# Attention output in transposed form: values stationary in four column groups, probabilities normalised before they stream

## The chip, the cores and the metric

The kernel runs on one core of one Trainium2 chip. Its time is the device time in microseconds; before, the median of three runs is 1509.24 us (1506.75 to 1510.07). Engines: PE (TensorE), DVE (VectorE), ACT (ScalarE), POOL (GpSimd), and SP, whose queue issues the large DMAs.

## What is computed

64 graphs of 128 nodes with 384 features, and one weighted 128x128 adjacency matrix each. Layer 0 is an attention with 12 heads of 32 channels, layer 1 is a graph network of two inner layers. Cut to what matters:

```
h = maximum(layernorm(x), 0)
q, k = h @ Wq.T, h @ Wk.T ;  v = h @ Wv.T + bv          # 12 heads of 32
s = q k^T * 384**-0.5 + 2 * adj
s = where(any(s != 0 in the row), s, -inf)
p = nan_to_num(softmax(s))
x = x + (p v) @ Wo.T + bo
h = maximum(layernorm(x), 0)
for l in 0, 1:
    u = h W_l h^T / sqrt(384), one matrix left of the diagonal's side, another on the other side
    delta = exp(u) * adj
    ctx = (delta / (sum(delta) + 1e-10)) @ (h @ W_lin.T + b_lin)
    h = relu(layer_norm(ctx))
x = x + h
```

## The kernel before, in words

Two graphs (j = 0, 1) form a group of 256 tokens; 32 groups follow each other. Every matrix product of full size is made from two parts: an operand is held as a high part and a low remainder, and three products (high-high, high-low, low-high) are summed in PSUM. So each PSUM result is read twice, by ACT, which writes the high part (L483), and by DVE, which subtracts it and writes the low part (L585).

The steps of one group, by name: T1a, T1b transpose the normed input; QK0 to QK2 give queries and keys, V0, V1 the values; S{j}{a} are scores, four row groups a of 32 rows each, three heads in each; x{j}{a} are the exponentials of S{j}{a} on ACT (L507), 3 of 128x128 each; ph{j}{b} and pl{j}{b} split half b of the probabilities into two float16 parts (L515, L697); pth, ptl are DMA transposes of these parts on SP's queue; PV{j} multiplies them with the values (L415); OT{j} transposes the result (L422); WO{j} is the output projection. Then ln2, T2a, T2b, and for each inner layer l: N{l}0 to N{l}2 (six 256-column products in three steps), HL{l}{j}, U{l} (the scores), the chain U{l}.m, .w, .e, .d, .dh, .dl that makes delta and its two parts on DVE and ACT, C{l}{j} (the product with delta, which needs delta's low part), gst and gag (statistics), z, and HTa, HTb (transposes to the next inner layer).

The order on each engine is written by hand in the table ORDER: a row (step, ahead) says for which group a step is done while group g is at hand. Each engine works through its list strictly in that order, for g = 0 to 31. So attention of group g+1 runs beside the graph network of groups g and g-1. PSUM has eight banks, and BANK says which steps share one, in turn; a PE step waits until the step before it in its bank is drained.

Before, the exponentials stay unnormalised. PV{j} has the turned probabilities as its stationary operand (128x128) and streams 33 columns for each head: 32 values and a column of ones, whose result is the row's sum. DVE then takes the reciprocal of 12 sums (PV.r, PV.n) and scales (PV.o, L689), into o_sb, with nodes in the partitions; OT turns it. `prob`, the float32 buffer of the exponentials, exists once and serves j = 0 and j = 1 in turn.

Of the kernel before, what the change touches and what calls it, by code (L numbers as in the profile page):

```python
# [61 lines left out]
def w_lin(l):  # L62
# [9 lines left out]
    0: ["N12", "S00", "HL00", "QK2"],  # L72
    1: ["HL11", "C11", "T1a", "U0", "V1"],
    2: ["WO1", "T2a", "S10", "QK0", "WO0"],
    3: ["N10", "S03", "S12", "QK1", "HTa"],
    4: ["HL10", "S02", "S11", "PV0", "PV1", "HTb"],
    5: ["N11", "S01", "N02", "HL01", "OT0", "OT1"],
    6: ["T2b", "AT", "C10", "N00", "T1b", "C00"],
    7: ["U1", "N01", "S13", "C01", "V0"],
# [791 lines left out]
```

## Time and profile before

| | us |
|---|---|
| median of 3 runs | 1509.24 |
| the profiled execution, own time | 1507.34 |
| its span, first to last instruction | 1505.4 |
| PE busy | 1432.3 |
| DVE busy | 1243.8 |
| ACT busy | 903.5 |
| POOL busy | 508.9 |

Busy times are the union of an engine's instructions. The timelines used below merge instructions that follow each other: the first number is the start, the second the length. Instructions of one engine overlap a little at their ends, so what a step costs its engine is the distance from its start to the next start, where no idle time is noted in brackets.

### The profile page before, as it was taken

The page shows a single profiled execution, that of the slowest core. Times are in us where ns is not written, and L with a number is a line of the kernel's source. Part 1 is how long each engine was busy: PE and PEld are TensorE (multiplying, and loading weights), DVE is VectorE, ACT ScalarE, POOL GpSimd, SP SyncE. Part 2 cuts the span into 40 slices and gives each one's busy share as a digit, 9 for nine tenths or more (in the row PEclk, how much of TensorE's full clock was granted, in tenths as well). Part 3 has the DMA queues.
Part 4 walks back from the last instruction along what each step waited for, and adds up shares of the span by engine and source line. Part 5 has one row for each costly group of instructions (what it writes and reads, how often), then busy time and mean ns, then how long its engine had stood idle before and what let it go on. Part 6 is the DMA issues. An engine that isn't in the chain of part 4 may idle for free.

```text
span 1505.4 us, 40241 instructions
## 1 busy us (share of the span) xinstructions
PE 1432.3 (95%) x14464; PEld 1396.4 (93%) x14464; DVE 1243.8 (83%) x4619; ACT 903.5 (60%) x2027; POOL 508.9 (34%) x921
## 2 busy tenths in 40 slices
PE   3699999999999999999999999999999999999874
PEld 3599999999999999999999999999999999999874
DVE  5578988888888888888888888888888888888853
ACT  4566665656666556666565666656666665566531
POOL 4113333233334233343323333333333342333321
PEclk8799999999999999999999999999999999999996
DMA  6232322223221223232222333222223222232200
GB/s 216 54 57 58 68 42 62 48 64 68 57 62 43 55 60 64 58 67 50 55 50 61 68 57 68 41 57 53 64 68 57 56 49 57 58 64 57 54 12 11
DMA packets 235683, 89.39 MB, mean 59 GB/s; under 512 B 206784, under 2 KB 235200, under 8 KB 235488
## 3 DMA queue, kind: packets, MB, share of 16 engines
q1 hardware_dynamic: 234912, 85.63, 26.9%
q8 instruction: 119, 1.95, 0.5%
q0 software_dynamic: 576, 1.18, 0.3%
q14 instruction: 76, 0.62, 0.2%
HBM read 23.86 MB, written 12.58 MB: 24 GB/s over the span
## 4 chain that ended last, share of the span: by engine, by line
PE 92%; DVE 2%; DMA 2%; ACT 1%; issue 1%; POOL 1%; SPq 0%; DVEq 0%; POOLq 0%; ACTq 0%
PE bank L342 79%; PE bank L348 4%; PE bank L415 4%; PE bank L403 3%; PE bank L422 1%; DMA x_sb<-x 1%; DMA pT<-prob_parts 1%; PE bank L434 0%; ACT prob L507 0%; SPq L323 0%; DVE weights L570 0%; ACT xn L490 0%; DVE stats_ln L598 0%; ACT prob_parts L515 0%; ACT work L556 0%
## 5 line engine op out<-in xcount | busy, mean ns | idle before, releaser
L342 PE MATMUL bank<-h,weights 128*128 128x256 f32 x3456 | 425.1, 280 | 3.0 <-DVE h L750 3.0
L342 PEld LDWEIGHTS bank<-h,weights 128*128 128x128 f32 x3456 | 411.9, 190 | 3.8 <-issue 3.7
L507 ACT ACTIVATE prob<-prob,rmin 128x128 f32<-128x128 f32 x768 | 244.2, 393 | 3.4 <-DVE rmin L665 3.4
L342 PE MATMUL bank<-weights,h 128*128 128x384 f32 x1152 | 227.5, 342 | 0.0
L342 PE MATMUL bank<-hA,weights 128*128 128x256 f32 x1728 | 219.2, 283 | 1.4 <-DVE hA L585 1.4
L342 PEld LDWEIGHTS bank<-hA,weights 128*128 128x128 f32 x1728 | 212.1, 190 | 1.7 <-DVE hA L585 1.7
L342 PEld LDWEIGHTS bank<-weights,h 128*128 128x128 f32 x1152 | 194.3, 188 | 6.3
L483 ACT ACTIVATE n<-bank 128x512 fp32r<-128x512 f32 x192 | 113.7, 592 | 141.7 <-PE bank L342 141.0
L800 POOL TENSOR_SCALAR less_mean_gnn<-mv_gnn 128x2 f32<-128x2 f32 x64 | 32.9, 513 | 429.9 <-DVE mv_gnn L590 429.9
L665 DVE CUSTOM_DVE_ANT_0 prob<-bank,adj_sb 128x128 f32<-128x128 f32 x768 | 171.0, 286 | 0.2 <-issue 0.2
L585 DVE TENSOR_TENSOR n<-bank,n 128x512 fp32r<-128x512 f32 x192 | 128.9, 684 | 33.8 <-ACT n L483 28.9
L342 PE MATMUL bank<-n,h 128*128 128x256 f32 x1152 | 153.1, 287 | 0.3 <-DVE n L585 0.3
L342 PEld LDWEIGHTS bank<-n,h 128*128 128x128 f32 x1152 | 142.0, 191 | 1.0 <-issue 1.0
L787 POOL TENSOR_SCALAR less_mean_ln<-mv_ln 128x2 f32<-128x2 f32 x64 | 20.7, 324 | 358.0 <-DVE mv_ln L590 358.0
L697 DVE TENSOR_TENSOR prob_parts<-prob,prob_parts 128x768 f16<-128x768 f32 x128 | 118.2, 943 | 5.7 <-ACT prob_parts L515 5.6
L342 PE MATMUL bank<-weights,oT 128*128 128x384 f32 x576 | 115.8, 346 | 0.3 <-DVE oT L585 0.3
L342 PE MATMUL bank<-weights,hA 128*128 128x384 f32 x576 | 115.8, 345 | 0.0
L515 ACT ACTIVATE prob_parts<-prob 128x768 f16<-128x768 f32 x128 | 108.0, 844 | 3.1
L820 POOL TENSOR_TENSOR x_sb<-x_sb,bo_all 128x384 f32<-128x384 f32 x64 | 69.5, 1087 | 115.1 <-ACT xn L490 109.8
L342 PEld LDWEIGHTS bank<-weights,oT 128*128 128x128 f32 x576 | 101.2, 190 | 0.5 <-issue 0.5
L585 DVE TENSOR_TENSOR hl<-bank,hl 128x384 fp32r<-128x384 f32 x128 | 70.6, 552 | 34.2 <-ACT hl L483 34.2
L342 PEld LDWEIGHTS bank<-weights,hA 128*128 128x128 f32 x576 | 97.4, 188 | 0.0
(101 smaller groups left out, 2453.8 us busy)
## 6 DMA issues: line engine op xcount, KB each, us to landing
x_sb<-x SPq DMA_DIRECT2D x32, 384.0 KB, 3.2
out<-x SPq DMA_DIRECT2D x32, 384.0 KB, 2.7
adj_sb<-adj SPq DMA_DIRECT2D x32, 128.0 KB, 2.1
pT<-prob_parts SPq DMA_TRANSPOSE x256, 2.8
x<-w SPq DMA_DIRECT2D x3, 576.0 KB, 4.8
pT<-w SPq DMA_DIRECT2D x3, 576.0 KB, 6.6
prob<-w SPq DMA_DIRECT2D x2, 576.0 KB, 7.3
prob_parts<-w SPq DMA_DIRECT2D x2, 576.0 KB, 6.0
```

The costliest lines, as they stand in the source:

```text
L342: mm = pe.matmul(out, lhsT, rhs, start=(n == 0), stop=(n == len(pairs) - 1))
L348: mm = pe.transpose(bank(job)[:, n * T + j * P:n * T + (j + 1) * P], src[:, j, c * P:(c + 1) * P], ident[:, :])
L403: mm = pe.matmul(bank(f"S{j}{a}")[:, c * P:(c + 1) * P], qk[rs, g % 2, u, c, js], qk[rs, g % 2, v, C + c, js], start=(n == 0), stop=(n == ...
L415: mm = pe.matmul(bank(step)[:, h * DA:(h + 1) * DA], pT[:, a, h % HC * C + h // HC, :], v2[:, b, j, h, :], start=(h == 0 and n == 0), stop ...
L483: act.activation(out, src, ACT.Copy).then_inc(s_hi, 1)
L507: e = act.activation(prob[:, a * C + h // HC, :], prob[:, a * C + h // HC, :], ACT.Exp, bias=rmin[:, j, h:h + 1], scale=-1.0)
L515: act.activation(pp[:, HI, hs, :], prob[:, hs, :], ACT.Copy).then_inc(s_part[HI][b], 1)
L585: dve.tensor_tensor(out, src, hi_part if hi_part.dtype == F16 else hi_part.bitcast(F32), ALU.subtract).then_inc(free(job), 1)
L665: r = dve.tensor_tensor_reduce(prob[:, a * C + c, :], bank(step)[:, c * P:(c + 1) * P], adj_sb[:, p, j, :], -2.0, 3.0e38, ALU.add, ALU.min ...
L697: dve.tensor_tensor(pp[:, LO, hs, :], prob[:, hs, :], pp[:, HI, hs, :], ALU.subtract).then_inc(s_part[LO][b], 1)
L800: pool.tensor_scalar(less_mean["gnn"][:, :], mv["gnn"][:, :, 0], -1.0, None, ALU.mult)
L820: pool.tensor_tensor(x_sb[:, p, j, :], x_sb[:, p, j, :], bo_all[:, :], ALU.add).then_inc(s_xbo[j], 1)
```

## The change

PV{j} is turned round. The values of a head (128x32) become the stationary operand, written to 32 of the 128 PSUM partitions, so that the four heads a of one c occupy four column groups; the turned probabilities stream, 128 columns. The result has channels in the partitions, which is the form that OT made, so OT{j} is left out; ACT and DVE split the PV result straight into oT. As the sum of a row can't be applied to this form afterwards, the probabilities are scaled before: each exponential also writes its sum (accum_out), DVE's new step nr{j}{b} takes the reciprocals of six sums, and ph{j}{b} first scales six 128x128 tiles on ACT, waits for them, and then writes the high part. The scale carries a factor -128, which the weight Wo takes back. The column of ones goes. The tables BANK and ORDER are new throughout.

```diff
@@ BANK, ORDER, SPLIT_AFTER: new tables; one line of the SP list
-        ("ld_x", 2), ("ld_adj", 2), ("pth01", 1), ("pth00", 1), ("ptl00", 1), ("ptl01", 1), ("pth10", 1), ("ptl10", 1),
+        ("ld_x", 2), ("ld_adj", 2), ("pth01", 1), ("ptl01", 1), ("pth00", 1), ("ptl00", 1), ("pth10", 1), ("ptl10", 1),
...
@@ PE
-                    for h in range(NH):
-                        for n, (a, b) in enumerate(PARTS):
-                            mm = pe.matmul(bank(step)[:, h * DA:(h + 1) * DA], pT[:, a, h % HC * C + h // HC, :], v2[:, b, j, h, :],
-                                           start=(h == 0 and n == 0), stop=(n == 2), skip_group_check=True)
-                    mm.then_inc(full(step), 1)
-                elif step[:2] == "OT":
-                    j = int(step[2])
-                    wait_drained(pe, f"PV{j}", g)
+
                     for c in range(C):
-                        mm = pe.transpose(bank(step)[:, c * P:(c + 1) * P], o_sb[:, j, c * P:(c + 1) * P], ident[:, :])
+                        for n, (u, w) in enumerate(PARTS):
+                            for a in range(HC):
+                                mm = pe.matmul(bank(step)[a * D:(a + 1) * D, c * P:(c + 1) * P], v2[:, w, j, c * HC + a, :], pT[:, u, a * C + c, :],
+                                               start=(n == 0), stop=(n == len(PARTS) - 1))
                     mm.then_inc(full(step), 1)
...
@@ ACT
-                        e = act.activation(prob[:, a * C + h // HC, :], prob[:, a * C + h // HC, :], ACT.Exp, bias=rmin[:, j, h:h + 1], scale=-1.0)
+                        e = act.activation(prob[:, a * C + h // HC, :], prob[:, a * C + h // HC, :], ACT.Exp, bias=rmin[:, j, a * C + h // HC:a * C + h // HC + 1], scale=-1.0,
+                                           accum_out=exp_sum[:, j, a * C + h // HC:a * C + h // HC + 1])
                     e.then_inc(s_exp[j][a], 1)
                 elif step[:2] == "ph":
                     j, b = int(step[2]), int(step[3])
                     hs = slice(2 * b * C, 2 * (b + 1) * C)
-                    for a in (2 * b, 2 * b + 1):
-                        act.wait_ge(s_exp[j][a], g + 1)
+                    act.wait_ge(s_nrm[j][b], g + 1)
+                    for i in range(2 * b * C, 2 * (b + 1) * C):
+                        e = act.activation(prob[:, i, :], prob[:, i, :], ACT.Copy, scale=rinv[:, j, i:i + 1])
+                    e.then_inc(s_scaled[j][b], 1)
                     ge(act, s_turned[HI][b], 16 * (G * g + j))
+                    act.wait_ge(s_scaled[j][b], g + 1)
                     act.activation(pp[:, HI, hs, :], prob[:, hs, :], ACT.Copy).then_inc(s_part[HI][b], 1)
...
@@ DVE
-                elif step[:2] == "PV":
...
+                elif step[:2] == "nr":
+
+                    j, b = int(step[2]), int(step[3])
+                    hs = slice(2 * b * C, 2 * (b + 1) * C)
+                    dve.wait_ge(s_row0[j], g + 1)
+                    for a in (2 * b, 2 * b + 1):
+                        dve.wait_ge(s_exp[j][a], g + 1)
+                    dve.scalar_tensor_tensor(out=row0[:, j, hs], in0=exp_sum[:, j, hs], scalar=float(P), in1=row0[:, j, hs],
+                                             op0=ALU.is_equal, op1=ALU.mult)
+                    dve.reciprocal(rinv[:, j, hs], exp_sum[:, j, hs]).then_inc(s_recip[j][b], 1)
+                    dve.wait_ge(s_recip[j][b], g + 1)
+                    dve.scalar_tensor_tensor(out=rinv[:, j, hs], in0=row0[:, j, hs], scalar=-P_SCALE, in1=rinv[:, j, hs],
+                                             op0=ALU.add, op1=ALU.mult).then_inc(s_nrm[j][b], 1)
```

What the new order does at two places. First PE, from U0 to HTb. Before, U0 is the block into bank1 from n2, then come PV0, QK0, QK1, and the two C blocks (hl, dT):

```order
L342 MATMUL bank1<-n2,h0 128x256 x18
L415 MATMUL bank4<-v2,pT 128x33 x36
L342 MATMUL bank2<-hA,weights 128x256 x18
L342 MATMUL bank3<-hA,weights 128x256 x18
L342 MATMUL bank6<-hl,dT 128x386 x3
L342 MATMUL bank7<-hl,dT 128x386 x3
L342 MATMUL bank0<-hA,weights 128x256 x18
L422 MATMUL bank5<-ident,o_sb 128x128 x3
```

After, PE from U0 (bank6 from n2), QK0, PV0, C01, C00, QK2, QK1, V0, WO0, PV1:

```order
L346 MATMUL bank6<-n2,h0 128x256 x18
L346 MATMUL bank2<-hA,weights 128x256 x18
L421 MATMUL bank4<-pT,v2 32x128 x36
L346 MATMUL bank1<-hl,dT 128x386 x3
L346 MATMUL bank7<-hl,dT 128x386 x3
L346 MATMUL bank6<-hA,weights 128x256 x18
L346 MATMUL bank1<-hA,weights 128x256 x18
L346 MATMUL bank5<-weights,hA 128x384 x9
L346 MATMUL bank3<-weights,oT 128x384 x9
L421 MATMUL bank1<-pT,v2 32x128 x36
```

Between U0 and the C blocks there is one QK block now where there were two; the OT transposes are gone.

The second place is ACT, the steps of graph j = 1. Before, from x{1}{.} to the splits of the QK blocks, the exponentials stand in threes between other steps:

```order
L507 ACTIVATE prob<-prob,rmin 128x128 x3
L483 ACTIVATE hl<-bank5 128x384
L483 ACTIVATE hA<-bank6 128x256
L507 ACTIVATE prob<-prob,rmin 128x128 x3
L515 ACTIVATE prob_parts<-prob 128x768
L507 ACTIVATE prob<-prob,rmin 128x128 x3
L540 ACTIVATE work<-work 128x256
L507 ACTIVATE prob<-prob,rmin 128x128 x3
L515 ACTIVATE prob_parts<-prob 128x768
```

After, on ACT, from x12 to ph11; L515 are now the scale copies and L519 the high parts:

```order
L507 ACTIVATE prob,exp_sum<-prob,rmin 128x128 x3
L483 ACTIVATE hA<-bank2 128x256
L483 ACTIVATE hl<-bank1 128x384
L554 ACTIVATE c_sb<-c_sb,shift_gnn,scale_gnn 128x384 x2
L483 ACTIVATE hA<-bank5 128x512
L507 ACTIVATE prob,exp_sum<-prob,rmin 128x128 x9
L483 ACTIVATE hl<-bank3 128x384
L545 ACTIVATE work<-work 128x256
L515 ACTIVATE prob<-prob,rinv 128x128 x6
L519 ACTIVATE prob_parts<-prob 128x768
L515 ACTIVATE prob<-prob,rinv 128x128 x6
L519 ACTIVATE prob_parts<-prob 128x768
```

Both ph steps have moved behind the last exponential, since their scales need the sums, and each has six scale copies ahead of it. On DVE, the order from U0 on is now U0.m, r01, U0.w, nr10, nr11, HL01, U0.d, U0.dh, U0.dl; before, it had no step there that needs an exponential other than pl10.

On DVE before, the steps after U1 are U1.m, U1.w, S01, U1.d, U1.dh, HL11, U1.dl, S03, S02, S00. After, they are U1.m, U1.w, S02, T2b, U1.d, S01, U1.dh, S03, U1.dl, HL11, S00, r00, nr01, N01, C11, nr00, C10, gst11, gst10, pl01, gag1, S12, S13, pl00, N02, N00, S11, S10, T1b, T1a, HL00. ACT's list beside it, after T2b and xn1_1: U1.e, x02, HL11, AT, x01, x03, N01, x00, ph01, ph00, N02, N00, x12, T1b, HL00, z1_0, z1_1, T1a, x11, x10, x13, HL01, U0.e, ph10, ph11.

## Rows read from the trace of the kernel before

**Rows 1.** The page: busy time by engine, and the chain by engine.

```profile
PE 1432.3 (95%) x14464; PEld 1396.4 (93%) x14464; DVE 1243.8 (83%) x4619; ACT 903.5 (60%) x2027; POOL 508.9 (34%) x921
...
PE 92%; DVE 2%; DMA 2%; ACT 1%; issue 1%; POOL 1%; SPq 0%; DVEq 0%; POOLq 0%; ACTq 0%
```

**Rows 2.** Windows view: 20 groups; clock, DMA share and GB/s come last.

```profile
300.00:1185.60 885.60, 884.50 (x9040) 865.15 (x9039) 765.73 (x2881) 555.39 (x1260) 313.51 (x560) 1.00 0.28 58
```

**Rows 3.** Timeline of PE: start us, us, engine, line, operation, count.

```profile
709.14 1.07 PE L415 MATMUL bank<-v,pT 128*128 128x33 f16 x36
710.06 4.49 PE L342 MATMUL bank<-hA,weights 128*128 128x256 f32 x36
...
717.57 0.49 PE L422 MATMUL bank<-ident,o_sb 128*128 128x128 f32 x3
717.82 1.82 PE L342 MATMUL bank<-weights,hA 128*128 128x384 f32 x9
...
736.79 0.68 PE L403 MATMUL bank<-qk 32*128 32x128 f16 x36
737.40 1.83 PE L342 MATMUL bank<-weights,h 128*128 128x384 f32 x9
...
753.39 1.06 PE L415 MATMUL bank<-v,pT 128*128 128x33 f16 x36
```

**Rows 4.** Timeline of ACT, the stretch with AT, x, splits, z1, ph.

```profile
740.26 0.38 ACT L530 ACTIVATE adjT<-bank 128x256 f32<-128x256 f32 x1
740.53 2.74 ACT L507 ACTIVATE prob<-prob,rmin 128x128 f32<-128x128 f32 x9
743.16 0.58 ACT L483 ACTIVATE n<-bank 128x512 fp32r<-128x512 f32 x1
743.64 0.84 ACT L515 ACTIVATE prob_parts<-prob 128x768 f16<-128x768 f32 x1
...
749.68 1.31 ACT L549 ACTIVATE c_sb<-c_sb,shift_gnn,scale_gnn 128x384 f32<-128x384 f32 x2 [1.84 <-POOL shift_gnn L809]
750.89 0.47 ACT L483 ACTIVATE hl<-bank 128x384 fp32r<-128x384 f32 x1
751.27 0.98 ACT L507 ACTIVATE prob<-prob,rmin 128x128 f32<-128x128 f32 x3
...
752.52 0.37 ACT L483 ACTIVATE hA<-bank 128x256 fp32r<-128x256 f32 x1
```

**Rows 5.** Timeline of DVE: PV1.r and PV1.n; U1.m to U1.dl; HL01.

```profile
720.66 0.17 DVE L680 SCALAR_TENSOR_TENSOR row<-bank,row 128x12 f32<-128x12 f32 x1 [0.90 <-PE bank L415]
...
721.01 0.17 DVE L685 SCALAR_TENSOR_TENSOR rinv<-row,rinv 128x12 f32<-128x12 f32 x1
...
737.00 0.69 DVE L724 TENSOR_TENSOR work<-bank,mask 128x512 f32<-128x512 f32 x1 [0.43 <-PE bank L342]
737.72 0.43 DVE L727 TENSOR_TENSOR work<-work 128x256 f32<-128x256 f32 x1
738.07 0.28 DVE L665 CUSTOM_DVE_ANT_0 prob<-bank,adj_sb 128x128 f32<-128x128 f32 x1
...
738.71 0.42 DVE L730 TENSOR_TENSOR work<-work,adjT 128x256 f32<-128x256 f32 x1
739.16 0.29 DVE L733 CAST dT<-work 128x256 fp32r<-128x256 f32 x1
...
740.28 0.41 DVE L736 TENSOR_TENSOR dT<-work,dT 128x256 fp32r<-128x256 f32 x1
...
752.17 0.55 DVE L585 TENSOR_TENSOR hl<-bank,hl 128x384 fp32r<-128x384 f32 x1
```

**Rows 6.** Groups by line and shape: busy us, mean ns.

```profile
L515 ACT ACTIVATE prob_parts<-prob 128x768 f16<-128x768 f32 x128 | 108.0, 844 | 3.1
...
L665 DVE DVE_READ_ACCUMULATOR2_ANT rmin<- 128x1 f32 x768 | 63.9, 83 | 0.0
...
L502 ACT ACTIVATE v<-v_sum 128x384 f16<-128x384 f32 x64 | 33.7, 527 | 30.9 <-DVE v_sum L654 30.9
```

More of the change, by code:

```diff
@@ L51 @@
 WQ, WK, WV, WO = range(4)
+P_SCALE = 128.0
+W_SCALE = {WQ: Q_SCALE, WK: K_SCALE, WO: -1 / P_SCALE}
 def w_left(l):
@@ L71 @@
 BANK = {
[L72 to L79, printed above, removed]
+    0: ["S03", "S11"],
+    1: ["WO1", "U1", "C10", "HL00", "C01", "QK1", "PV1"],
+    2: ["S01", "T1b", "QK0"],
+    3: ["N11", "T2a", "HL11", "C11", "S13", "HL01", "WO0"],
+    4: ["S02", "N02", "PV0", "HTb"],
+    5: ["N10", "N12", "T2b", "N01", "S12", "T1a", "V0", "HTa"],
+    6: ["HL10", "S00", "N00", "U0", "QK2"],
+    7: ["AT", "S10", "C00", "V1"],
 }
@@ L83 @@
     "SP": [
[1 row of a table removed]
[1 row of a table added]
         ("pth11", 1), ("ptl11", 1), ("out", -1)],
     "PE": [
[5 rows of a table removed]
-    "ACT": [
[5 rows of a table removed]
[5 rows of a table added]
+    "ACT": [
[5 rows of a table added]
         ("HTa", 0)],
     "DVE": [
[9 rows of a table removed]
[9 rows of a table added]
     "POOL": [
-        ("ln2", 0), ("ln1", 2), ("xbo0", 2), ("ml", 0), ("xbo1", 2), ("gn1", -1), ("mu", 0), ("za0", -1), ("za1", -1),
-        ("zb0", -1), ("zb1", -1), ("gn0", 0)],
+        ("ln2", 0), ("ln1", 2), ("xbo0", 2), ("mu", 0), ("ml", 0), ("xbo1", 2), ("gn1", -1), ("za0", -1), ("za1", -1),
+        ("zb1", -1), ("zb0", -1), ("gn0", 0)],
 }
 SPLIT_JOBS = (["T1a", "T1b", "QK0", "QK1", "QK2",
-              "OT0", "OT1", "T2a", "T2b"] + [f"N{l}{k}" for l in range(L) for k in range(3)] +
+              "PV0", "PV1", "T2a", "T2b"] + [f"N{l}{k}" for l in range(L) for k in range(3)] +
               [f"HL{l}{j}" for l in range(L) for j in range(G)])
@@ L168, in build @@
         v_sum = sb("v_sum", [P, G, H])
-        v2 = sb("v2", [P, 2, G, NH, DA], F16)
+        v2 = sb("v2", [P, 2, G, NH, D], F16)
         prob = sb("prob", [P, NH, P])
@@ L177, in build @@
         row0 = sb("row0", [P, G, NH])
+        exp_sum = sb("exp_sum", [P, G, NH])
         rinv = sb("rinv", [P, G, NH])
@@ L223, in build @@
         s_row0 = [sem(f"row0_{j}") for j in range(G)]
-        s_recip = [sem(f"sum_inverse{j}") for j in range(G)]
-        s_rinv = [sem(f"negated_inverse{j}") for j in range(G)]
+        s_recip = [[sem(f"sum_inverse{j}{b}") for b in range(2)] for j in range(G)]
+        s_nrm = [[sem(f"prob_scale{j}{b}") for b in range(2)] for j in range(G)]
+        s_scaled = [[sem(f"prob_scaled{j}{b}") for b in range(2)] for j in range(G)]
         s_mask = [sem("mask_left"), sem("mask_right")]
@@ L245, in build @@
         SPLIT_AFTER = {
-            "ACT": {"": (0,), "xn1_1": (1,), "T1b": (2, 3), "QK1": (4, 5), "QK0": (6,), "QK2": (7,), "V0": (8,), "V1": (9,)},
-            "DVE": {"ln1_ag": (0,), "T1b": (1, 2), "QK1": (3, 4), "QK0": (5,), "QK2": (6, 7), "V0": (8,), "V1": (9,)}}
+            "ACT": {"": (0,), "xn1_1": (1,), "T1a": (2, 3), "QK0": (4, 5), "QK2": (6,), "QK1": (7,), "V0": (8,), "V1": (9,)},
+            "DVE": {"ln1_ag": (0,), "T1a": (1, 2), "QK0": (3, 4), "QK2": (5,), "QK1": (6, 7), "V1": (8,), "V0": (9,)}}
         def staged(m):
@@ L412, in run @@
                             pe.wait_ge(s_turned[part][b], 16 * (G * g + j + 1))
[L413 to L420 removed]
                     for c in range(C):
[L422 removed]
+                        for n, (u, w) in enumerate(PARTS):
+                            for a in range(HC):
+                                mm = pe.matmul(bank(step)[a * D:(a + 1) * D, c * P:(c + 1) * P], v2[:, w, j, c * HC + a, :], pT[:, u, a * C + c, :],
+                                               start=(n == 0), stop=(n == len(PARTS) - 1))
                     mm.then_inc(full(step), 1)
                 elif step[:2] == "WO":
[L425 removed]
+                    wait_drained(pe, f"PV{step[2]}", g)
                     rows(step, g, WO, oT, 0)
@@ L475, in split_weights @@
                     wait_load(act, m)
-                    act.activation(W[:, m, HI, :, :], staged(m), ACT.Copy, scale={WQ: Q_SCALE, WK: K_SCALE}.get(m, 1.0)).then_inc(s_whi, 1)
+                    act.activation(W[:, m, HI, :, :], staged(m), ACT.Copy, scale=W_SCALE.get(m, 1.0)).then_inc(s_whi, 1)
             def hi(job, grp, out, cols, pattern=None, **kw):
@@ L511, in run @@
                     hs = slice(2 * b * C, 2 * (b + 1) * C)
-                    for a in (2 * b, 2 * b + 1):
-                        act.wait_ge(s_exp[j][a], g + 1)
+                    act.wait_ge(s_nrm[j][b], g + 1)
+                    for i in range(2 * b * C, 2 * (b + 1) * C):
+                        e = act.activation(prob[:, i, :], prob[:, i, :], ACT.Copy, scale=rinv[:, j, i:i + 1])
+                    e.then_inc(s_scaled[j][b], 1)
                     ge(act, s_turned[HI][b], 16 * (G * g + j))
+                    act.wait_ge(s_scaled[j][b], g + 1)
                     act.activation(pp[:, HI, hs, :], prob[:, hs, :], ACT.Copy).then_inc(s_part[HI][b], 1)
-                elif step[:2] == "OT":
-                    j = int(step[2])
+                elif step[:2] == "PV":
+                    wait_filled(act, *(("WO0", g) if step == "PV1" else ("WO1", g - 1)))
                     hi(step, g, oT[:, HI, :, :], H, "p (c q) -> p c q", c=C)
@@ L569, in split_weights @@
                     dve.wait_ge(s_whi, m + 1)
-                    dve.scalar_tensor_tensor(out=W[:, m, LO, :, :], in0=staged(m), scalar={WQ: Q_SCALE, WK: K_SCALE}.get(m, 1.0),
+                    dve.scalar_tensor_tensor(out=W[:, m, LO, :, :], in0=staged(m), scalar=W_SCALE.get(m, 1.0),
                                              in1=W[:, m, HI, :, :].bitcast(F32), op0=ALU.mult, op1=ALU.subtract).then_inc(s_wlo, 1)
@@ L697, in run @@
                     dve.tensor_tensor(pp[:, LO, hs, :], prob[:, hs, :], pp[:, HI, hs, :], ALU.subtract).then_inc(s_part[LO][b], 1)
-                elif step[:2] == "OT":
+                elif step[:2] == "PV":
                     lo(step, g, oT[:, LO, :, :], oT[:, HI, :, :], H, "p (c q) -> p c q", c=C)
@@ L755, in _ @@
                     split_weights(SPLIT_AFTER["DVE"].get(step, ()))
-                    if step == "QK0":
+                    if step == "QK2":
                         make_constants()
```

31 lines of the change are left out of this document (4 added, 27 removed), and 38 rows, old and new, of the table ORDER.

## The prediction

> **What bounds the kernel now.** I read the page's busy times and its chain first: TensorE is busy 95% of the span and 92% of the chain is TensorE [rows 1]. In the steady part it has 1.1 us without work in 885.6 us, at the full granted clock (1.00, its 2.4 GHz level), while VectorE is busy for 86% and ScalarE for 63% of it [rows 2]. So one group of two graphs costs what TensorE's instructions cost. The PE timeline gives the period: the same PV block starts at 709.14 and again at 753.39, 44.25 us apart [rows 3]. Thirty-two groups and a head and a tail make 1505.4 us. Next I read the timelines of ACT and DVE for what a step costs from its start to the next one's start, since the change gives these two engines work and puts three engines near their limits. All sums below are per group and are then set against the profiled execution's own 1507.3 us, 1.9 us under the median of the runs.
>
> **TensorE: what goes.** A PV block takes 0.92 us before (709.14 to 710.06), 36 matmuls of 33 columns with a 128x128 stationary each. Its new form has 36 matmuls too, 32-column stationaries in four column groups and 128 columns streaming. No row shows column groups; the nearest is the S block, 36 matmuls of 128 columns in four row groups, 0.61 us (736.79 to 737.40) [rows 3]. I take 0.61. From below, the same block can't be much faster than the S block, since both stream the same columns; from above it is four times as slow as overlap gives, below among the rivals. The OT transposes go: 0.25 us a block (717.57 to 717.82) [rows 3]. Two graphs: 2 x 0.31 + 2 x 0.25 = 1.12 us less, 43.13 us a group if TensorE stays gapless. That alone would be 30 x 1.12 = 34 us over the span (30 full groups is my count, with head and tail taken out).
 By it the sum would be a dearer PV block, at worst the 0.92 of before or rival 4; the gain on TensorE would shrink to the 0.50 of the transposes. The new stationaries are a quarter as wide, so I leave the 0.61.
>
> **ScalarE: what comes.** (a) 24 scale copies of 128x128 with a pointer scale. The exponentials have the same shape and one pointer too (the bias): nine take 2.63 us from start to start (740.53 to 743.16), 0.292 us each [rows 4]. Six cost 1.75 us. (b) In each of the four ph steps the copy now waits for the last scale's end: 0.13 us (the overlap of 0.10 lost, and a semaphore). With its own 0.75 us, a ph step costs 2.63 us. (c) 24 exponentials also give their sum. No row shows this on ScalarE. On VectorE the same thing is an instruction of its own, 83 ns long [rows 6], and it hides: three reductions with their reads take 0.64 us (738.07 to 738.71) [rows 5]; so the lower bound is 0. From above, two copies of 384 and 768 elements take 527 and 844 ns [rows 6]: 0.83 ns an element and 210 ns fixed, of which about 100 ns overlap with the next one; so 0.11 us of engine time for an instruction that moves one element, and 0.21 us if nothing overlaps. I call this price r and take 0.06, half way between hidden and 0.11, since the two nearest rows are the ends. Together 7.0 + 0.5 + 24 r = 9.0 us more on an engine that had 16.5 us idle a group. It fits in total; the question is where.
> The 83 ns row is an instruction of its own on VectorE. The Trainium skill (VectorE: DVE Perf Modes, Two Vector instructions with no wait between them) counts an operation with an accumulator output as two instructions, and says so of VectorE alone. If it held for ScalarE with the fixed part unhidden, r would be the 0.11 of the upper row, not 0.
>
> **VectorE.** PV.r, PV.n, PV.o of two graphs go; four nr steps come. One costs what the three small operations cost, 0.52 us (720.66 to the end of the one at 721.01) [rows 5]. 4 x 0.52 against 2 x (0.52 + 0.55): nothing in total. But they are placed in the middle of the chains.
>
> **The stretch that decides.** I walk from the end of U1 on PE (t = 0, in the trace 736.79) to C01, in the new order. PE: from there to the end of U0 are the same blocks as in 736.79 to 753.39, 16.60 us, and T2b, 0.15: U0 ends at 16.75. Then QK0 (2.16) and PV0 (0.61): PE reaches C01 at 19.52. In the order before, two QK blocks stand there.
> ACT and DVE: U1.m starts at 0.21, U1.w at 0.93, S02 at 1.28, its three take 0.64 and the read's end 0.08 [rows 5]: x02 can start at 2.0. From there ACT has, without a gap: 8 x steps of 0.88, HL11 and HL01's predecessor HL00 at 0.38 each, AT 0.27, the splits N01, N02, N00 and T1a at 0.48 each, T1b 0.27, the two z1 1.21 and the steps ph01 and ph00 at 2.63 [rows 4]: 7.04 + 0.76 + 0.27 + 1.92 + 0.27 + 1.21 + 5.26 = 16.73 us. The last exponential, x13, ends at 2.0 + 16.73 + 0.15 = 18.9, 2.1 us after U0. In DVE's order nr11, which needs it, stands before the chain of U0.d: nr11 0.52, HL01 0.47, U0.d 0.42, U0.dh 0.32, U0.dl 0.41, semaphores 0.1 [rows 5]: delta's low part is there at 21.15. PE waits 1.63 us at C01, and behind it on PE's queue stand QK2, QK1, V0 and WO0, all of them blocks that would have had their data. The way from C01 round to the end of U1 is 43.13 - 19.52 = 23.61 us of PE work; I find no late operand on it (pl11 and its turns land about 1 us before PV1; HTa's split about 0.5 us before N10). Period: 21.15 + 23.61 = 44.76 us, and all 24 sums lie on this walk before x13, so 44.76 + 24 r. With r = 0.06 it is 46.2, 1.95 more than 44.25; 30 x 1.95 = 59; 1507.3 + 59 = **1566 us**.
>
> **Rivals.** (1) The sum is hidden (r = 0): period 44.76, 30 x 0.51 = 15 more: 1523 us. For it: VectorE's own read hides. (2) The ScalarE is never late. Then from U0's end the DVE chain is 0.21 + 0.72 + 0.43 + 2 x 0.47 for nr10 and nr11 + 0.47 + 0.42 + 0.32 + 0.41 = 3.9 us against PE's 2.77: a wait of 1.15 us eats the 1.12 saved: 1508 us, no change. (3) Faster: PE keeps its cover, because the steps cost DVE and ACT some 10% less than my rows say, or U0's chain starts earlier by way of the banks; down to PE's own 43.13: 1473 us, and half of it 1490. For it: PE, the bound now, does get 1.12 us less. Against it: two separate walks put C01 later. It decides at a delta that is ready 19.5 us after U1. (4) The column groups don't overlap. A 256-column matmul costs 0.12 us (18 in 2.16), so 128 columns 0.06, a block 2.16. PV0's hides in the wait at C01 to 1.63 us, PV1's doesn't: 1.55 x 30 = 46 on top: 1612 us. (5) r = 0.2, near the ScalarE's whole fixed part: 49.6, 160 more: 1667 us.
>
> **How the numbers follow.** Chances: the walk with r between 0.03 and 0.12 (1545 to 1610), 0.50; rival 1, 0.20; rival 2, 0.08; rival 3, 0.14; rivals 4 and 5 together 0.08. A difference of 0.2%, 3 us, is about what a measurement of this kernel tells from none: slower 0.50 + 0.20 + 0.08 = 0.78, same 0.08, faster 0.14. The range leaves out the lower part of rival 3 and most of 4 and 5: 1490 to 1620 us.
>
> **What would show it.** In the changed profile: PV block 0.6 us from start to start; no transposes of o_sb by the OT line; PE idle before the C matmuls of layer 0, released by DVE dT, 1.5 to 3 us a group, with the PE sum at 43.1; ACT busy near 37 us a group and gapless from x02 to ph11; a row for ScalarE's accumulator read, or a mean of an exponential above 393 ns, gives r. Wrong, if PE shows no idle at C01 or DVE reaches nr11 with its exponentials long done.

## The result and the profile after

The changed kernel takes 1614.76 us (median of 4 runs, 1613.15 to 1615.83), against 1508.29 (1506.75 to 1510.07) for the kernel before in the same comparison: 1.0705 times as long, 95% interval 1.0686 to 1.0723. It is slower by 106.5 us, where 59 were forecast. The direction and the chain that was forecast came out; the size did not. Each ratio below is to the kernel before as measured beside that run (medians 1506.76 to 1508.37).

The page of the kernel after, its first section and its chain; they answer to [rows 1], where TensorE had 95% of the span and 92% of the chain:

```profile
PE 1444.8 (90%) x14272; PEld 1367.9 (85%) x14272; DVE 1281.1 (79%) x4747; ACT 1195.0 (74%) x3563; POOL 493.2 (31%) x919
...
PE 46%; ACT 36%; DVE 10%; issue 3%; DMA 3%; SPq 1%; POOL 1%; DVEq 0%; ACTq 0%; POOLq 0%
```

The chain is now shared: TensorE 46%, ScalarE 36%, VectorE 10%. The same steady stretch as in [rows 2] (busy time of PE, PEld, DVE, ACT, POOL, then the granted clock) has 55 us without TensorE work, where it had 1.1:

```profile
340.00:1225.60 885.60, 830.31 (x8277) 787.94 (x8276) 730.12 (x2733) 680.09 (x2042) 280.66 (x519) 0.99 0.26 54
```

TensorE's timeline, from the first S block behind U1 (t = 0 of the forecast's walk) to PV0, C01, and round to the next such block; it answers to [rows 3]:

```profile
740.65 0.68 PE L407 MATMUL bank<-qk 32*128 32x128 f16 x36
741.26 1.84 PE L346 MATMUL bank<-weights,h 128*128 128x384 f32 x9
...
758.98 2.36 PE L346 MATMUL bank<-hA,weights 128*128 128x256 f32 x18 [0.60 <-issue]
761.26 0.69 PE L421 MATMUL bank<-pT,v 128*32 128x128 f16 x36
763.89 1.30 PE L346 MATMUL bank<-hl,dT 128*128 128x386 f32 x6 [1.94 <-DVE dT L734]
765.03 4.40 PE L346 MATMUL bank<-hA,weights 128*128 128x256 f32 x36
...
772.54 0.69 PE L421 MATMUL bank<-pT,v 128*32 128x128 f16 x36
...
788.03 0.68 PE L407 MATMUL bank<-qk 32*128 32x128 f16 x36
```

The turned PV block is 0.69 us long (0.61 to 0.62 from start to start where its successor follows at once, as in e5 and e9 below), as the S block is. C01 waits 1.94 us for delta's low part on VectorE. The group takes 788.03 - 740.65 = 47.38 us; before, 44.25 [rows 3].

ScalarE and VectorE in front of that wait, start and length; they answer to [rows 4, 5]. ScalarE, from the start of x02 over the scale copies of ph01 and ph00 to x13 and HL01:

```profile
742.46 0.40 ACT L507 ACTIVATE prob<-prob,rmin 128x128 f32<-128x128 f32 x1 [0.23 <-DVE rmin L669]
...
748.22 1.86 ACT L515 ACTIVATE prob<-prob,rinv 128x128 f32<-128x128 f32 x6
...
750.92 1.85 ACT L515 ACTIVATE prob<-prob,rinv 128x128 f32<-128x128 f32 x6
...
760.73 0.40 ACT L507 ACTIVATE prob<-prob,rmin 128x128 f32<-128x128 f32 x1
761.02 0.20 ACT L507 ACTIVATION_READ_ACCUMULATOR prob<-prob,rmin 128x1 f32 x1
761.12 0.40 ACT L507 ACTIVATE prob<-prob,rmin 128x128 f32<-128x128 f32 x1
761.41 0.20 ACT L507 ACTIVATION_READ_ACCUMULATOR prob<-prob,rmin 128x1 f32 x1
761.50 0.48 ACT L483 ACTIVATE hl<-bank 128x384 fp32r<-128x384 f32 x1
```

VectorE:

```profile
760.54 0.94 DVE L684 SCALAR_TENSOR_TENSOR row<-exp_sum,row 128x6 f32<-128x6 f32 x1
...
761.74 0.17 DVE L684 SCALAR_TENSOR_TENSOR row<-exp_sum,row 128x6 f32<-128x6 f32 x1
...
762.12 0.55 DVE L590 TENSOR_TENSOR hl<-bank,hl 128x384 fp32r<-128x384 f32 x1
762.59 0.42 DVE L728 TENSOR_TENSOR work<-work,adjT 128x256 f32<-128x256 f32 x1
763.04 0.29 DVE L731 CAST dT<-work 128x256 fp32r<-128x256 f32 x1
763.37 0.43 DVE L734 TENSOR_TENSOR dT<-work,dT 128x256 fp32r<-128x256 f32 x1
```

x13, the last exponentials, end with their last read at 761.61; nr11 starts at 761.74, and behind it HL01, U0.d, U0.dh, U0.dl run without a gap until TensorE starts C01 at 763.89. ScalarE has no gap from 742.46 on; a ph step takes 2.70 us (748.22 to 750.92), where 2.63 was forecast. This is the chain of the forecast, step for step. The read is an instruction of its own on ScalarE: 0.20 us long, and 760.73 to 761.12 is 0.39 us from one exponential to the next, where it was 0.292 [rows 4]. Exactly (nine of them): 0.385, so r = 0.093 us. The groups by shape (busy us, mean ns, idle before), which answer to [rows 6]:

```profile
L507 ACT ACTIVATE prob<-prob,rmin 128x128 f32<-128x128 f32 x768 | 297.9, 397 | 8.1 <-DVE rmin L669 8.0
L515 ACT ACTIVATE prob<-prob,rinv 128x128 f32<-128x128 f32 x768 | 237.6, 393 | 0.0
L507 ACT ACTIVATION_READ_ACCUMULATOR prob<-prob,rmin 128x1 f32 x768 | 150.5, 196 | 0.0
...
L407 PEld LDWEIGHTS bank<-qk 32*128 32x128 f16 x2304 | 33.8, 94 | 22.9 <-issue 19.0
L421 PEld LDWEIGHTS bank<-pT,v 128*32 128x32 f16 x2304 | 33.3, 97 | 15.7 <-issue 11.6
...
L684 DVE SCALAR_TENSOR_TENSOR row<-exp_sum,row 128x6 f32<-128x6 f32 x128 | 44.1, 345 | 17.8 <-ACT prob L507 16.6 <-DVE row L676 0.9 <-issue 0.3
```

The last row was not foreseen: an operation on six columns with a mean of 345 ns, and 0.94 us at 760.54. Nor was a second thing. Not all groups take 47.4 us: of 19 in the steady part, 7 take 48.5 to 48.8. In six of them the granted clock falls behind the wait at C01; the seventh (382.01 to 430.54) runs at the full clock and has further waits of 0.44 us at PV1 and 0.66 at U1 instead. TensorE's timeline in one of the six, and two stretches of 12 us (the granted clock is the third number from the end), the first with that wait, the second with the wait at 763.89:

```profile
715.36 2.19 PE L346 MATMUL bank<-hl,dT 128*128 128x386 f32 x6 [2.02 <-DVE dT L734]
717.35 5.08 PE L346 MATMUL bank<-hA,weights 128*128 128x256 f32 x36
```

```profile
708.00:720.00 12.00, 9.39 (x93) 8.94 (x92) 10.92 (x36) 11.81 (x39) 4.23 (x4) 0.86 0.27 46
...
756.00:768.00 12.00, 9.46 (x105) 9.00 (x105) 10.92 (x40) 11.82 (x41) 4.23 (x4) 1.00 0.25 45
```

The two C blocks take 1.99 us instead of 1.14, the two QK blocks 4.92 instead of 4.24: part of this stretch ran at the 1.2 GHz level (1.00 is 2.4 GHz). The group costs 48.53 us (715.36 to 763.89), 1.1 more than its neighbours.

### The profile page after: what moved, and what is told of

Read it like the earlier page. It is cut to its first block, busy times and chain, and to the rows that moved or that the text cites. A ratio compares the mean times of both kernels' runs of the same rounds, so it can differ in the third digit from the quotient of the medians.

```text
span 1613.0 us, 41581 instructions
## 1 busy us (share of the span) xinstructions
PE 1444.8 (90%) x14272; PEld 1367.9 (85%) x14272; DVE 1281.1 (79%) x4747; ACT 1195.0 (74%) x3563; POOL 493.2 (31%) x919
## 4 chain that ended last, share of the span: by engine, by line
PE 46%; ACT 36%; DVE 10%; issue 3%; DMA 3%; SPq 1%; POOL 1%; DVEq 0%; ACTq 0%; POOLq 0%
PE bank L346 42%; ACT prob L507 16%; ACT prob L515 8%; ACT prob_parts L519 4%; ACT n L483 3%; PE bank L352 3%; ACT c_sb L554 2%; DVE row L684 2%; ACT hl L483 2%; ACT hA L483 1%; DVE work L722 1%; PE bank L421 1%; DMA x_sb<-x 1%; SPq L327 1%; DMA pT<-prob_parts 1%
## 5 line engine op out<-in xcount | busy, mean ns | idle before, releaser
L346 PE MATMUL bank<-h,weights 128*128 128x256 f32 x3456 | 431.3, 283 | 3.4 <-DVE h L748 2.3
L507 ACT ACTIVATE prob<-prob,rmin 128x128 f32<-128x128 f32 x768 | 297.9, 397 | 8.1 <-DVE rmin L669 8.0
L346 PEld LDWEIGHTS bank<-hA,weights 128*128 128x128 f32 x1728 | 217.8, 195 | 27.7 <-issue 24.0
L515 ACT ACTIVATE prob<-prob,rinv 128x128 f32<-128x128 f32 x768 | 237.6, 393 | 0.0
L669 DVE CUSTOM_DVE_ANT_0 prob<-bank,adj_sb 128x128 f32<-128x128 f32 x768 | 177.1, 286 | 0.4 <-issue 0.2
L796 POOL TENSOR_SCALAR less_mean_gnn<-mv_gnn 128x2 f32<-128x2 f32 x64 | 14.2, 222 | 475.9 <-DVE mv_gnn L595 475.9
L346 PE MATMUL bank<-hl,dT 128*128 128x386 f32 x384 | 91.1, 377 | 69.1 <-DVE dT L734 67.6
L507 ACT ACTIVATION_READ_ACCUMULATOR prob<-prob,rmin 128x1 f32 x768 | 150.5, 196 | 0.0
L346 PEld LDWEIGHTS bank<-hl,dT 128*128 128x128 f32 x384 | 69.5, 206 | 76.2 <-issue 74.3
L783 POOL TENSOR_SCALAR less_mean_ln<-mv_ln 128x2 f32<-128x2 f32 x64 | 14.1, 220 | 374.7 <-DVE mv_ln L595 374.7
L519 ACT ACTIVATE prob_parts<-prob 128x768 f16<-128x768 f32 x128 | 108.1, 845 | 11.6
```

Of the source, the lines that this page charges most:

```text
L346: mm = pe.matmul(out, lhsT, rhs, start=(n == 0), stop=(n == len(pairs) - 1))
L507: e = act.activation(prob[:, a * C + h // HC, :], prob[:, a * C + h // HC, :], ACT.Exp, bias=rmin[:, j, a * C + h // HC:a * C + h // HC + ...
L515: e = act.activation(prob[:, i, :], prob[:, i, :], ACT.Copy, scale=rinv[:, j, i:i + 1])
L519: act.activation(pp[:, HI, hs, :], prob[:, hs, :], ACT.Copy).then_inc(s_part[HI][b], 1)
L669: r = dve.tensor_tensor_reduce(prob[:, a * C + c, :], bank(step)[:, c * P:(c + 1) * P], adj_sb[:, p, j, :], -2.0, 3.0e38, ALU.add, ALU.min ...
```

## The experiments

"Group" is the mean distance of the C01 blocks of about 20 groups in the steady part; "undisturbed" is that of groups without the lower clock.

| kernel | us | ratio to before, 95% interval | group (undisturbed) | wait at C01 |
|---|---|---|---|---|
| before | 1508.29 | | 44.29 (44.2) | 0 |
| after | 1614.76 | 1.0686 to 1.0723 | 47.83 (47.4) | 1.94 to 2.02, once 2.37 |
| e1 no sums | 1581.83 | 1.0467 to 1.0498 | 46.76 (45.6) | 1.95 |
| e2 no scale copies | 1582.18 | 1.0469 to 1.0501 | 46.90 (45.7) | 1.96 |
| e3 neither | 1555.52 | 1.028 to 1.0334 | 46.01 (45.1) | 1.87 |
| e6 neither, no additions of ln_b | 1509.65 | 1.0002 to 1.0028 | 44.66 (44.3) | 1.02 |
| e12 after, no additions of ln_b | 1613.07 | 1.0675 to 1.0713 | 47.79 (47.3) | 1.95 |
| e4 before, PV turned | 1539.06 | 1.0185 to 1.0221 | 45.24 | 0 |
| e5 e4 drained earlier | 1528.68 | 1.0127 to 1.0157 | 45.00 | 0 |
| e9 e5, HL01 later, PV1 split before z0 | 1500.84 | 0.9931 to 0.997 | 44.10 | 0 |
| e7 before, with the sums | 1526.45 | 1.0112 to 1.0143 | 44.86 | 0 |
| e8 after, old order | 1939.18 | 1.2843 to 1.2888 | 58.0 | 2.94 |
| e10 high part from the scale copy | 1608.01 | 1.064 to 1.0682 | 47.52 (47.4) | 1.25 |
| e11 delta's chain first | 1707.48 | 1.129 to 1.1338 | 50.69 | 1.34 |

**What ScalarE's new work costs: e1, e2, e3.** e1 leaves out the sums, e2 the scale copies and the wait behind them, e3 both.

```diff
@@ e1
-                        e = act.activation(..., ACT.Exp, ..., scale=-1.0,
-                                           accum_out=exp_sum[:, j, a * C + h // HC:a * C + h // HC + 1])
+                        e = act.activation(..., ACT.Exp, ..., scale=-1.0)
@@ e2
-                    for i in range(2 * b * C, 2 * (b + 1) * C):
-                        e = act.activation(prob[:, i, :], prob[:, i, :], ACT.Copy, scale=rinv[:, j, i:i + 1])
-                    e.then_inc(s_scaled[j][b], 1)
...
-                    act.wait_ge(s_scaled[j][b], g + 1)
```

> The changed kernel without the sums: the exponentials write none, so the 24 accumulator reads a group are gone; the scale copies stay and take their factor from sums fixed at 1. Theory A (ScalarE's queue is on the walk from U1 to C01, and each read lengthens it by the 0.093 us that it adds from start to start): 24 x 0.093 = 2.2 us a group less, 33 groups: 74 us, 1541 us. Theory B (the new tables of order and banks are at fault, ScalarE has room, 74% busy): within 10 us of 1615.

> The changed kernel without the 24 scale copies a group and without the wait behind them; sums and reciprocals stay, the probabilities are not divided. Theory A: of 4 x 1.88 us, the two of graph 0 lie on the walk U1 to C01, 3.8 us; what then ends last is VectorE's own chain behind U0, so not all of it comes back: a group 44.3 to 44.7 us, 1510 to 1530 us. Theory B: within 10 us of 1615.

> The changed kernel without both, sums and scale copies, in its new order. Theory A: ScalarE is never late; PE 43.1 us a group, and a wait of about 1.15 us at C01 for VectorE's chain behind U0 with two nr steps in it: 44.3 us, 1505 to 1520 us. Theory C (the new order itself costs nothing, PE would be gapless): 43.1 us, 1475 us. Theory B: above 1580 us.

None of the three came out as its theory A said: 1582 us against 1541, 1582 against 1510 to 1530, 1556 against 1505 to 1520. But e1 and e2 each take 33 us away, and e3 59, so ScalarE's new work is on the path. An undisturbed group falls by 1.8 us in e1, where 24 r = 2.2 was expected. ScalarE and VectorE in e1, in front of a C01 that starts at 465.77:

```profile
459.92 2.74 ACT L507 ACTIVATE prob<-prob,rmin 128x128 f32<-128x128 f32 x9
...
462.40 0.98 DVE L683 SCALAR_TENSOR_TENSOR row<-exp_sum,row 128x6 f32<-128x6 f32 x1
...
463.62 0.17 DVE L683 SCALAR_TENSOR_TENSOR row<-exp_sum,row 128x6 f32<-128x6 f32 x1
```

x13 ends at 462.66, but nr11 starts only at 463.62: without the sums VectorE is the late one, held by nr10, whose first operation takes 0.98 us. The time falls by less still, since 13 of 19 groups now have the lower clock. In e3 ScalarE is no longer late, but C01 still waits 1.87 us, not the 1.15 of VectorE's chain alone. The missing 0.8 us are one long VectorE operation in a group: in most groups nr10's first (the first row below is the mean over all four nr steps of a group; in e6 it is 162 ns, and (341 - 162) x 128 = 23 us are 0.8 us in some 28 groups), in a few U0.w (second row). Then GpSimd beside that U0.w (the products with ln_a and the additions of ln_b, two of each):

```profile
L679 DVE SCALAR_TENSOR_TENSOR row<-exp_sum,row 128x6 f32<-128x6 f32 x128 | 43.7, 341 | 3.5 <-ACT prob L507 1.8 <-DVE row L671 0.3 <-issue 0.3
```

```profile
733.68 1.26 DVE L720 TENSOR_TENSOR work<-work 128x256 f32<-128x256 f32 x1
```

```profile
730.59 2.00 POOL L826 TENSOR_TENSOR c_sb<-c_sb,lna_all 128x384 f32<-128x384 f32 x2 [0.82 <-ACT c_sb L549]
732.67 1.99 POOL L830 TENSOR_TENSOR c_sb<-c_sb,lnb_all 128x384 f32<-128x384 f32 x2
```

U0.w takes 1.26 us instead of 0.43 and ends at 734.94, 0.28 after GpSimd's addition ends at 734.66. The 0.94 us of nr10 in the kernel after end at 761.48, beside a GpSimd addition that ends at 761.46. The Trainium skill (SBUF — State Buffer, SBUF: two separate sides) says that a VectorE operation with two SBUF inputs and a GpSimd operation that reads SBUF share a port pair as an exclusive lock, held for a whole instruction. By that rule each row is what one would expect, and the traces agree: 0.94 us instead of 0.17, 1.26 instead of 0.43.

**Whether that collision is the cause: e6 and e12.** The same omission in e3 and in the changed kernel:

```diff
-                    pool.tensor_tensor(c_sb[:, j, :], c_sb[:, j, :], lnb_all[:, :], ALU.add).then_inc(s_zb[j], 1)
+                    pool.engine_nop().then_inc(s_zb[j], 1)
```

> As e3 (the changed kernel without sums and scale copies), and POOL's two additions of lnb (128x384, about 1 us each) left out; their signals stay. In e3 DVE's U0.w or the first operation of nr10 takes 0.9 us longer than elsewhere while these additions run. Theory E (the two engines hinder each other there, and it is on the path to C01): that operation falls to its usual length, the wait at C01 from 1.9 to about 1.1 us, a group 45.1 to 44.3 us, and fewer groups fall to half clock: 1520 to 1530 us. Otherwise: 1555 us as e3.

> This is the changed kernel with one thing left out: GpSimd's additions of ln_b (L834), so its output is not the reference's. The scale copies and the read accumulators stay. In the kernel without sums and scaling the same omission took 46 us. Theory A (the additions only cost where VectorE is the late one; in the changed kernel ScalarE's chain up to x13 is): VectorE's nr11 starts at 761.74, right behind x13's end at 761.61, so the 0.8 us that its operation beside GpSimd loses are hidden, and only the small waits ahead move: at most 0.5 us a group, 1598 to 1613 us, with the wait at C01 still 1.5 us or more. Rival B (VectorE's lost time is on the path here too, and the groups with a half clock go with it): 0.8 us in each of 33 groups and some of the half-clock groups, 1570 to 1585 us, wait at C01 about 1.1.

e6, then e12 (TensorE's timeline, and in e12 the group of nr's first operation):

```profile
760.62 1.30 PE L346 MATMUL bank<-hl,dT 128*128 128x386 f32 x6 [1.02 <-DVE dT L729]
```

```profile
668.07 1.30 PE L346 MATMUL bank<-hl,dT 128*128 128x386 f32 x6 [1.95 <-DVE dT L734]
...
L684 DVE SCALAR_TENSOR_TENSOR row<-exp_sum,row 128x6 f32<-128x6 f32 x128 | 21.1, 165 | 44.2 <-ACT prob L507 40.3 <-DVE row L676 0.9
```

In e6 the wait falls to 1.02 and the time by another 46 us, to that of before: 0.85 us of the wait in some 30 groups are 26, and the lower clock is gone from the steady part (granted clock 1.00 from 340 to 1225 us, mean of the run 0.977 as before). In e12 the collision goes as well (345 ns become 165, VectorE's idle time there that exponentials end grows from 16.6 to 40.3 us), and the time stays: in the kernel after the long operation ends at 761.48, and x13 only at 761.61. So the collision, with the lower clock that comes with the longer wait, costs 46 us where VectorE is the late one, and next to nothing where ScalarE is late as well. In e6 a group without its wait is 44.3 - 1.02 = 43.3 us, 0.9 less than before, and the wait for VectorE's chain behind U0 eats it: this is the forecast's rival 2, with its 1508 us. That the two nr steps in that chain are what makes it late was read from the rows; no run moves them alone.

**What the turned product is worth by itself: e4, e5, e9.** The order of before, with the turned PV, without OT and without any division. In e4 PV drains where OT did; e5 gives oT a second place and drains each PV sooner on VectorE's list; e9 also moves HL01 behind U0 on TensorE and ScalarE, and lets ScalarE split PV1 ahead of z0.

```diff
@@ e4, PE
-                    for h in range(NH):
...
+                    for c in range(C):
+                        for n, (u, w) in enumerate(PARTS):
+                            for a in range(HC):
+                                mm = pe.matmul(bank(step)[a * D:(a + 1) * D, c * P:(c + 1) * P], v2[:, w, j, c * HC + a, 0:D], pT[:, u, a * C + c, :],
@@ e5, ACT
-("QK1", 2), ("QK0", 2), ("PV0", 1),
+("PV0", 1), ("QK1", 2), ("QK0", 2),
@@ e9, PE
-("S13", 1), ("HL01", 0), ("T1b", 2), ("U0", 0), ("PV0", 1),
+("S13", 1), ("T1b", 2), ("U0", 0), ("HL01", 0), ("PV0", 1),
@@ e9, ACT
-("z0_1", 0), ("z0_0", 0), ("PV1", 1), ("HTb", 0),
+("PV1", 1), ("z0_1", 0), ("z0_0", 0), ("HTb", 0),
```

> The kernel before, in its own order and banks, with PV alone turned round (values stationary in four column groups, turned probabilities streaming) and OT left out; no sums and no division, so PV.r, PV.n and PV.o are gone too. Theory A: PE stays the bound and is 1.1 us a group shorter: 36 us, 1472 us. Theory D (column groups don't overlap well, or a switch of the array's form costs): 1508 us or more.

> As e4 (kernel before, PV turned round, no sums and no division, no OT), with what made e4 wait mended: a second place for the turned output, so that ACT can split PV1 before WO0 has run, and DVE drains PV0 ahead of QK1 and PV1 ahead of WO0. Theory A (the turned form itself saves 1.1 us a group on PE): no PE wait, a group 43.1 to 43.3 us, 1470 to 1476 us. Theory D (there is a cost of the turned form beyond those waits): above 1490 us.

> As e5, with cover given back to the chain C00, statistics, POOL, z0, HTb, on which e5 waits 1.3 us a group: PE does HL01 behind U0 and no longer ahead of it, and ACT splits PV1 ahead of z0. No sums, no division. Theory F (e4 and e5 were slow because OT and the longer PV blocks had covered just this chain): no PE wait, 43.1 to 43.4 us a group, 1468 to 1480 us. Theory D (the turned form costs something of its own): above 1500 us.

The theory that TensorE gets its 34 us or more failed in all three, and all three times lie where theory D (a cost of the turned form itself) had put them, e9's only just. But the rows don't show such a cost: the block stays 0.69 us long, and TensorE waits elsewhere. TensorE's timeline of e4; then in e5 ScalarE (z0, PV1's high part), VectorE (PV1's low part) and TensorE (HTb); then TensorE of e9:

```profile
733.47 0.69 PE L416 MATMUL bank<-pT,v 128*32 128x128 f16 x36 [0.43 <-DVE oT L581]
737.15 0.88 PE L348 MATMUL bank<-ident,c_sb 128*128 128x128 f32 x6 [1.21 <-DVE oT L581]
```

```profile
729.35 1.31 ACT L526 ACTIVATE c_sb<-c_sb,shift_gnn,scale_gnn 128x384 f32<-128x384 f32 x2 [2.33 <-POOL shift_gnn L772]
730.56 0.47 ACT L464 ACTIVATE h<-bank 128x384 fp32r<-128x384 f32 x1
731.06 0.56 DVE L567 TENSOR_TENSOR h<-bank,h 128x384 fp32r<-128x384 f32 x1 [2.64 <-ACT h L464]
731.67 0.87 PE L334 MATMUL bank<-ident,c_sb 128*128 128x128 f32 x6 [1.30 <-DVE h L567]
```

```profile
718.12 0.84 PE L329 MATMUL bank<-ident,c_sb 128*128 128x128 f32 x6 [0.38 <-ACT c_sb L521]
...
759.68 0.69 PE L397 MATMUL bank<-pT,v 128*32 128x128 f16 x36 [0.40 <-DMA pT<-prob_parts]
```

In e4 PV1 and HTb wait for the draining of a bank. In e5 HTb still does: it shares a bank with PV1, ScalarE splits PV1 only behind z0, and HTb starts when VectorE's low part ends at 731.62, although z0 had ended at 730.66 and TensorE was free at 730.38. So about 1 us of the 1.3 is the draining and 0.3 the way to z0. That way, from the start of the first C block over statistics, GpSimd's small operations and z0, takes 7.6 us in e5 (723.04 to 730.66). Before, it takes the same (714.39 to 722.00), under 8.01 us of TensorE's work, in which the OT blocks and the longer PV1 stood, 0.9 us together; ScalarE's z0 and TensorE's HTb of the kernel before:

```profile
720.69 1.31 ACT L544 ACTIVATE c_sb<-c_sb,shift_gnn,scale_gnn 128x384 f32<-128x384 f32 x2 [1.61 <-POOL shift_gnn L809]
...
722.40 0.82 PE L348 MATMUL bank<-ident,c_sb 128*128 128x128 f32 x6
```

With 0.4 us to spare, taking out 0.9 leaves HTb short of cover. e9 has PV1 drained in time, and there HTb waits for z0 itself, 0.38 us. HL01 does not stand between C and HTb, so it adds nothing to that cover; which of e9's two moves brought the 28 us over e5 wasn't told apart. e9 is the fastest kernel of all, and still gains 7 us instead of the 34 that the shorter blocks are worth; its waits alternate between HTb and the turned probabilities, 0.45 us a group, and the other half microsecond stands in small gaps that weren't followed up. And it does no division at all.

**The sums in the kernel before, and the old order: e7, e8.** e7 is the kernel before with the sums written on ScalarE and not used; e8 is the changed arithmetic in the order and banks of before, with nr and ph put in by hand.

```diff
@@ e7
-..., bias=rmin[:, j, h:h + 1], scale=-1.0)
+..., bias=rmin[:, j, h:h + 1], scale=-1.0,
+                                           accum_out=exp_sum[:, j, h:h + 1])
@@ e8, ORDER["DVE"]
-("C11", -1), ("C10", -1),
+("r00", 1), ("C11", -1), ("nr01", 1), ("C10", -1), ("nr00", 1),
```

> The kernel before, whole, with one thing added: each exponential also writes its sum (24 accumulator reads a group), which nothing uses. Theory A (it costs 0.093 us each, but only where ScalarE is on the path; before it has 16 us a group idle, 1.8 of it behind graph 0's exponentials and 1.2 behind graph 1's): within 3 us of 1508. Rival (each read costs the kernel wherever it stands): 24 x 0.093 x 33 = 74 us, 1580 us.

> The whole new arithmetic (sums, nr steps, scale copies, turned PV, no OT) in the order and the banks of before, nr and ph moved only as far as the sums need. Theory B (the new tables are at fault): well under 1600 us, towards 1520. Theory A (the 9.7 us that ScalarE gets a group lie between S and PV in any order of one group a period): 46.5 to 47.5 us a group, 1580 to 1620 us.

e7 fell between the theories: some 19 us. ScalarE has room for 2.2 us a group, but the probabilities come later and PV waits for their turns. Its row, where the kernel before has 10.1 us of such waits:

```profile
L416 PE MATMUL bank<-v,pT 128*128 128x33 f16 x2304 | 68.5, 178 | 17.5 <-DMA pT<-prob_parts 17.2
```

That is 7 of the 19 us; the rest is spread over small gaps and wasn't followed up. e8 is out of both ranges by far. Its waits (us in total, times, longest) show each half of the probabilities passed to and fro between ScalarE and VectorE with both waiting:

```profile
DVE prob_parts L680 <- ACT prob_parts L504: 167.6, 96, 2.9
...
ACT prob L500 <- DVE rinv L673: 149.5, 64, 3.0
```

So the old order, with nr and ph put in this way, is far worse than the new tables; a better placement in it may exist, and one placement doesn't acquit the new tables. What speaks for them is e6: in the new order, without ScalarE's new work and the collision, the kernel takes the time of before.

**Two attempts to mend it: e10, e11.** e10 writes the float16 high part straight from the scaled copy and leaves the product with rinv to VectorE's low part; e11 puts HL01 and the chain of delta ahead of x13 and nr11.

```diff
@@ e10, ACT and DVE
+                        e = act.activation(pp[:, HI, i, :], prob[:, i, :], ACT.Copy, scale=rinv[:, j, i:i + 1])
...
-                    dve.tensor_tensor(pp[:, LO, hs, :], prob[:, hs, :], pp[:, HI, hs, :], ALU.subtract)
+                        e = dve.scalar_tensor_tensor(out=pp[:, LO, i, :], in0=prob[:, i, :], scalar=rinv[:, j, i:i + 1],
+                                                     in1=pp[:, HI, i, :], op0=ALU.mult, op1=ALU.subtract)
@@ e11, ORDER["ACT"]
-("T1a", 2), ("x11", 1), ("x10", 1), ("x13", 1), ("HL01", 0), ("U0.e", 0),
+("T1a", 2), ("HL01", 0), ("x11", 1), ("x10", 1), ("U0.e", 0), ("x13", 1),
```

> The changed kernel, whole result, but the six scale copies of a ph step write the float16 high part themselves: the copy of 768 elements and the wait behind the scales go (4 x 0.88 us of ScalarE a group, two of them between U1 and C01), and DVE makes the low part in six operations, about 0.4 us more for each pl. Theory A (ScalarE's queue from x02 to x13 sets the group): 1.4 to 1.8 us a group less, 45.5 to 46.2 us and some groups at half clock: 1555 to 1580 us. Rival (VectorE is as near to the bound as ScalarE, its 1.6 us more take it back): 1600 us or more.

> The changed kernel, whole result, in another order: ACT does HL01 ahead of x11 and U0.e ahead of x13; DVE does nr11 behind U0.dl and gag0 ahead of pl11; PE does PV1 behind V1, and WO1 behind N10. The arithmetic is the same. Theory A: C01 no longer hangs on x13; the walk U1 to C01 is 1.7 us shorter, the way by ph11, pl11 and PV1 then is as long as 44.5 to 45.5 us a group: 1545 to 1575 us. Rival (POOL's additions next to U0.w set it, whatever stands there): 1600 us or more.

e10 shortens the wait at C01 to 1.25 us and the undisturbed group stays at 47.39: waits at HTb (0.60), PV1 (0.35) and U0 (0.55) take it back, as the rival said; that VectorE's six operations for each half are behind them is read from its list, not tested. The 7 us that it gains are the lower clock, which is not seen in the steady part (1.00 from 340 to 1225 us). e11 failed: the wait at C01 falls to 1.34, but seven other places now wait 0.2 to 1.0 us, 5.4 us a group in all with C01. My forecast for it looked at one chain; which of the moved steps spoils most wasn't told apart. The collision with GpSimd isn't gone there either, it falls on U0.w, for example 1.17 us at 854.92.

## Why the prediction was right, and where its size went wrong

**TensorE's part** held for the blocks: 0.61 us for the turned PV block, no OT. Rival 4, that column groups don't overlap, is out. Of the slower weight load that was weighed beside it no cost is seen: the loads take 97 ns in the mean, those of the S block 94, and the block is as short. TensorE's sum did not come out: 47.38 less its four waits (0.33, 0.60, 1.94, 0.15) is 44.36 us, not 43.1, and only e6 comes near with 43.3.

**The walk** held. Forecast with the measured r: x13 ends at 18.9 + 24 x 0.093 = 21.1, C01 at 21.15 + 2.2 = 23.4, period 47.0. Measured from 740.65: 20.96, 23.24, 47.38. What the walk has wrong is TensorE's own arrival at C01: 761.26 + 0.61 is 21.2 us after t = 0, not 19.52, so its wait there is 1.94 us and not the 23.4 - 19.5 = 3.9 that the walk implies. Waits at HL01 (0.33) and QK0 (0.60) and small gaps ahead of C01, which were not foreseen, make up the difference; they cost nothing, since they shorten the one at C01.

**The term that was mis-sized** is r. The forecast put it half way between hidden and 0.11 because VectorE's read hides; ScalarE's doesn't: of its 0.196 us, 0.093 stand on the path. The upper row was the nearer one. 24 x 0.033 x 30 = 24 us of the 49 missed. e1 shows that this term is on the path, until VectorE takes over; e7 that the reads cost some 19 us even in the order of before.

**What the forecast lacked**: from C01 round to U1's end TensorE takes 24.14 us, not 23.61 (0.15 us of wait behind PV1, and 0.2 more in the three blocks of N1, 777.20 to 783.55 against 726.21 to 732.33 before): 0.4 net of the earlier C01, 12 us. And the groups that take longer than 47.4: 47.83 on the mean, 13 us. The lower clock is most of that, 1.1 us in 6 of 19 groups, some 10 us. 24 + 12 + 13 = 49; the 30 groups were right (30 x 3.54 = 106).

**What was luck.** The forecast gave its own walk 1545 to 1610 us, and 1614.76 lies above that; the change is 1.8 times the 59 us. The time stands 5 us inside the stated range, 1490 to 1620, and only because that range reaches beyond the walk. Rival 4's 1612 us is the nearest number on the list, and its mechanism is not there.

**The rivals.** Rival 1 (sum hidden) and 5 (r = 0.2) are out by the rows. Rival 2 was the right account of what remains without ScalarE's work, with one thing more, the collision with GpSimd (e3, e6). Rival 3, that TensorE keeps its cover, is out even without the new work: of the 34 us, e9 realises 7. The forecast had counted TensorE's saving as certain and put the whole question into ScalarE; the rows of before, e5 and e9 show that the removed blocks were themselves cover for the chain from C to HTb, and e4 and e5 that the turned output must be drained in time.
